# The temperature polynomial of an entropy-adaptive attention, moved from GpSimd to VectorE

## The reference, cut to what matters

```python
original_probs = softmax(logits)
entropy = sum(-original_probs * log(original_probs + 1e-09))      # one number for each query row and head
e2 = entropy * entropy
poly_result = POLY[0]*e2*e2 + POLY[1]*e2*entropy + POLY[2]*e2 + POLY[3]*entropy + POLY[4]
beta = where(entropy > 0.5, maximum(poly_result, 1.0), 1.0)
attn = softmax(logits * beta)
```

## Time and profile before

| | |
|---|---|
| median of 3 runs | 1427.24 us (1426.59 to 1428.86) |
| span of the profiled execution | 1426.1 us |
| PE busy | 1279.1 us, 90% |
| DVE busy | 781.4 us, 55% |
| ACT busy | 729.5 us, 51% |
| POOL busy | 531.3 us, 37% |

### The profile page before, as it was taken

One profiled execution on the slowest core, in us unless ns is written; L12 is line 12 of the kernel. 1 busy time (PEld: TensorE's weight loads), 2 busy tenths in 40 slices (PEclk: granted clock), 3 DMA queues, 4 the chain that ended last, 5 costly groups with the idle time before them and its releaser, 6 DMA issues. The chain is left out here.

```text
span 1426.1 us, 25147 instructions
## 1 busy us (share of the span) xinstructions
PE 1279.1 (90%) x9396; PEld 1061.4 (74%) x9396; DVE 781.4 (55%) x1807; ACT 729.5 (51%) x1297; POOL 531.3 (37%) x745
## 2 busy tenths in 40 slices
PE   9899999989999999996788889888888888999995
PEld 7576776757999999995555656656666556999995
DVE  4886878774111111112665688986877655533332
ACT  6464756652322233221456677778767656444441
POOL 2113040402000000004797888878769223332222
PEclk9999999999999999998998999999999999999998
DMA  9674472901977777822100011010010615322221
GB/s 349 269 184 130 114 183 71 259 25 52 321 259 262 268 268 261 326 105 84 41 1 4 9 42 34 1 38 20 12 38 20 250 55 185 61 43 49 41 44 12
DMA packets 71272, 170.81 MB, mean 120 GB/s; under 512 B 8572, under 2 KB 47489, under 8 KB 61168
## 3 DMA queue, kind: packets, MB, share of 16 engines
q1 hardware_dynamic: 55520, 144.33, 31.5%
q0 software_dynamic: 10224, 16.09, 4.9%
q10 hardware_dynamic: 5408, 8.78, 1.7%
HBM read 122.78 MB, written 48.07 MB: 120 GB/s over the span
## 5 line engine op out<-in xcount | busy, mean ns | idle before, releaser
L1198 ACT ACTIVATE b_ht<-ps,b_b 128x154 f32<-128x154 f32 x256 | 85.3, 387 | 200.5 <-PE ps L1165 187.0
L1213 DVE TENSOR_SCALAR b_yt<-ps,b_b 128x154 f32<-128x154 f32 x64 | 21.2, 373 | 238.8 <-PE ps L1178 238.8
L2353 POOL DMA_INDIRECT experts<-ye,gidx_all x32 | 32.0, 1000 | 319.8 <-SPq L1104 309.3
L1165 PE MATMUL ps<-b_xet,ring 128*128 128x154 f32 x1024 | 141.1, 295 | 1.0 <-DVE b_xet L1206 1.0
L1178 PE MATMUL ps<-b_ht,ring 128*128 128x154 f32 x1024 | 139.7, 294 | 0.4 <-DVE b_yt L1213 0.4
L1178 PEld LDWEIGHTS ps<-b_ht,ring 128*128 128x128 f32 x1024 | 136.3, 189 | 0.6 <-issue 0.6
L1165 PEld LDWEIGHTS ps<-b_xet,ring 128*128 128x128 f32 x1024 | 135.7, 189 | 1.1 <-DVE b_xet L1206 1.1
L2637 POOL DMA_INDIRECT out_dram<-d_yd,d_to x39 | 60.8, 1558 | 146.7 <-DVE d_yd L2605 119.5
L1538 DVE TENSOR_REDUCE c_mx<-ps 128x8 f32<-128x1024 f32 x64 | 77.7, 1214 | 51.9 <-PE ps L1482 51.9
L2586 DVE TENSOR_TENSOR d_g<-d_gs,ps 128x512 f32<-128x512 f32 x37 | 25.4, 688 | 122.3 <-PE ps L2523 122.2
L1477 PE MATMUL ps<-experts 64*128 64x512 f32 x256 | 77.1, 674 | 16.3 <-ACT experts L1574 6.8
(11 more groups left out here) (345 smaller groups left out, 2969.3 us busy)
## 6 DMA issues: line engine op xcount, KB each, us to landing
ring<-in_w SPq DMA_DIRECT2D x64, 1024.0 KB, 5.3
xd<-zero SPq DMA_DIRECT2D x6, 3120.0 KB, 24.8
a_kp<-in_ctx_k SPq DMA_DIRECT2D x8, 1024.0 KB, 17.0
d_xd<-xd SPq DMA_DIRECT2D x39, 130.0 KB, 2.4
xe<-zero SPq DMA_DIRECT2D x1, 4928.0 KB, 35.2
b_xe<-xe SPq DMA_DIRECT2D x32, 154.0 KB
ye<-b_ye ACTq DMA_DIRECT2D x32, 154.0 KB
experts<-in_wd SPq DMA_DIRECT2D x1, 4608.0 KB
```

Of the source, the lines that this page charges most:

```text
L1165: r = pe.matmul(ps[:, b, CAP * (m % 2):CAP * (m % 2) + CAP], w1r[:, slot, k, P * m:P * m + P], xet[:, e % 2, k, :], start=(k == 0), stop=( ...
L1198: r = a.activation(ht[:, e % 2, m, :], ps[:, b, CAP * (m % 2):CAP * (m % 2) + CAP], ACT.Gelu, bias=b1[:, e, m:m + 1])
```

## The change

The nine operations on POOL and their place "po" in the order are gone. DVE does six fused operations on the same 128x8 tiles, written directly behind the sum L1807 in step "hr", so without an own due time. The algebra is (h + a) h + b for each factor instead of a h + b + h h, and the factor POLY[0] or zero is taken into the second factor. The tile `square` is gone. All other due times and the order of everything else stay. `be` is now raised by DVE; POOL's "db" waits for it as before.

```diff
             def unit(u):
                 v.wait_ge(*pr.at(g, u))
                 v.tensor_reduce(h, e[:, :, :], AX, ALU.add).then_inc(*hr.up())
+                p, (other, chosen) = po[u][:, :], (x[:, :] for x in gt[u])
+                v.wait_ge(*hr.at(g, u))
+                v.scalar_tensor_tensor(out=p, in0=h, scalar=FACTORS[0][0], in1=h, op0=ALU.add, op1=ALU.mult)
+                v.scalar_tensor_tensor(out=other, in0=h, scalar=FACTORS[1][0], in1=h, op0=ALU.add, op1=ALU.mult)
+                v.tensor_scalar(chosen, h, -0.5, POLY[0], ALU.is_lt, ALU.mult).then_inc(*c.dv.up())
+                v.wait_ge(*c.dv.now())
+                v.scalar_tensor_tensor(out=other, in0=other, scalar=FACTORS[1][1], in1=chosen, op0=ALU.add, op1=ALU.mult).then_inc(*c.dv.up())
+                v.wait_ge(*c.dv.now())
+                v.scalar_tensor_tensor(out=p, in0=p, scalar=FACTORS[0][1], in1=other, op0=ALU.add, op1=ALU.mult).then_inc(*c.dv.up())
+                v.wait_ge(*c.dv.now())
+                v.tensor_scalar(p, p, 1.0, None, ALU.max).then_inc(*be.up())
...
             def unit(u):
-                yield at("po", u)
-                pool.wait_ge(*hr.at(g, u))
-                pool.tensor_tensor(square, h, h, ALU.mult)
-                pool.tensor_scalar(p, h, *FACTORS[0], ALU.mult, ALU.add)
-                pool.tensor_scalar(other, h, *FACTORS[1], ALU.mult, ALU.add).then_inc(*c.po.up())
-                pool.tensor_scalar(chosen, h, -0.5, POLY[0], ALU.is_lt, ALU.mult)
-                pool.wait_ge(*c.po.now())
-                pool.tensor_tensor(p, p, square, ALU.add)
-                pool.tensor_tensor(other, other, square, ALU.add).then_inc(*c.po.up())
-                pool.wait_ge(*c.po.now())
-                pool.tensor_tensor(p, p, other, ALU.mult).then_inc(*c.po.up())
-                pool.wait_ge(*c.po.now())
-                pool.tensor_tensor(p, p, chosen, ALU.mult).then_inc(*c.po.up())
-                pool.wait_ge(*c.po.now())
-                pool.tensor_scalar(p, p, 1.0, None, ALU.max).then_inc(*be.up())
                 yield at("db", u)
                 pool.wait_ge(*be.at(g, u))
                 pool.tensor_tensor(d, d, wide(po[u]), ALU.mult).then_inc(*db.up())
```

More of the change, by code:

```diff
@@ L1627, in phase_c @@
         zz, en, po = ([sb("%s%d" % (name, u), [P, NU]) for u in range(len(UNITS))] for name in ("zz", "en", "po"))
-        gt = [[sb("%s%d" % (name, u), [P, NU]) for name in ("square", "other", "chosen")] for u in range(len(UNITS))]
+        gt = [[sb("%s%d" % (name, u), [P, NU]) for name in ("other", "chosen")] for u in range(len(UNITS))]
         x_rot, x_rms = [sb("x_rot%d" % n, [P, GS, D]) for n in range(2)], sb("x_rms", [P, GS, D])
@@ L1815, in unit @@
                 e, l, d = ent[u % 2][:, :, :], lnp[u % 2][:, :, :], one.d[u][:, :, :]
-                h, p, (square, other, chosen) = en[u][:, :], po[u][:, :], (x[:, :] for x in gt[u])
+                h, p, (other, chosen) = en[u][:, :], po[u][:, :], (x[:, :] for x in gt[u])
                 yield at("pn", u)
```

## The result

The changed kernel takes 1455.83 us (median of 4 runs, 1452.24 to 1458.67) against 1427.62 us of the kernel before (1426.59 to 1428.86): ratio 1.0194, 95% interval 1.0176 to 1.0213. It is slower by 28.2 us; the forecast was +2.1 and the range ended at 1436.0. A second comparison gave 1455.98 us and a ratio of 1.0211 (1.0173 to 1.0249). A trace is one execution, and those profiled end layer 0's expert tiles (last L1213), which no edit touches, anywhere from 651.0 to 655.5 us. Where traces of different kernels are compared over the whole span, I therefore also give the time from that point to the end: 774.7 us before, 799.5 in the changed kernel (797.9 in its second profile), 24.8 us more.

The account below looks back on a forecast made before the run. Engines were taken to bound the stage in turns, mostly DVE from 830 to 939 and POOL to 991. Terms -0.3 + 0.85 + 7.15 - 5.0 - 0.6 = +2.1 us gave 1429.3 us, range 1421.7 to 1436.

Parts of the forecast that it names:

- The toll of one polynomial: Six small DVE operations behind each sum L1807: 1.0 us per polynomial, bounds 0.55 and 1.57, 32 us of DVE in all.
- the slow rival: Rival B, 28%: DVE becomes the bound; one small operation of 1.85 us on top gives 1436 us.
- 695 to 830, +0.55: First stretch: -0.3 from POOL's gain, +0.85 from two sums at 763.68 ahead of L1918, which waited 1.15 us.
- 830 to 939, +6.1 up to the mark: Mostly DVE's path: sums cost +2.0, +2.5 and +1.0, L1730 +1.65; together +7.15 us for the whole stretch.
- the side effect: L1730 near 901: without the polynomial POOL runs a product beside its four operations, 3.45 instead of 1.79 us, +1.65.
- 939 to 991, -5.0: POOL on the path with four polynomials, 9.8 us; waits for DVE and ACT leave half of the gain, -5.0.
- rival B: 28%: DVE bounds the stage, deciding when the product at 968.80 waits for the reciprocal (slack 1.84 us); 1433.9 to 1436 us.
- 991 to 1110, -0.6: Last stretch: sum at 1021.93 on DVE's path +1.0, one polynomial on POOL's path -1.6; other sums covered by DVE idle.
- What is behind 1110: After the stage: no polynomial, so everything moves as a block by the shift with which the stage ends.
- One sign that I had named for it: After the change DVE between 830 and 947 should show almost no idle time.
- A: Rival, 22%: POOL's queue is the bound and DVE has room; -5.5 us in all, 1421.7 us.
- C: Rival, 10%: the change does nothing, gain and toll within 1 us or both beside a third engine's chain; 1427 us.

Follow-up runs that it names:

- the runs with reciprocals: Changed kernel, polynomial left out, reciprocals of 128x8 in place of the six VectorE operations: six per sum 1442.48 us, three 1430.09 us, six at the later step 1432.61 us.
- no polynomial: Kernel before with the polynomial left out on every engine (the factor is 1): 1425.25 us, ratio 0.9971.
- six reciprocals: Changed kernel with each of the six new VectorE operations replaced by a reciprocal of 128x8 in the same place, polynomial left out: 1442.48 us, ratio 1.0116.
- the later place: Six operations as their own VectorE step at the due time of GpSimd's old polynomial: changed kernel so altered 1441.82 us; the six-reciprocals kernel so altered 1432.61 us.
- the run with all kinds: Kernel without the polynomial, plus six independent 128x8 VectorE operations behind each sum, one of each kind in rotating order, results unused: 1455.19 us in one run.
- the run with halves: Changed kernel with each of GpSimd's three 128x1024 products in a unit issued as two of 128x512: 1451.46 us, ratio 1.0170.

## Why the prediction was wrong

The direction I thought a little likelier than its opposite came true, the size did not; the miss is 26.5 us, and the time lies 19.8 beyond the range.

Three terms of the sum failed. The toll of one polynomial was put at 1.0 us, and catching makes it 1.7 on average. The sums that pay it were counted as about eight, the others being taken as covered by idle time on VectorE; the runs with reciprocals give 17 to 21. And of the 5.0 us that GpSimd was to give back between 939 and 991 nothing came, since it waited for VectorE there.

The start of a sum on VectorE (L1807 and its counterparts), against its start in the kernel before, read from the timelines. Between these marks lie my four stretches; "forecast" is the running sum of the prediction up to there.

| sum that stood at | forecast | no polynomial | six reciprocals | changed kernel |
|---|---|---|---|---|
| 703.00 | 0 | +2.3 | +2.5 | -0.6 |
| 842.57 | +0.6 | -3.4 | +0.4 | +7.6 |
| 935.36 | +6.7 | +3.0 | +13.6 | +19.0 |
| 1013.00 | +2.7 | -1.5 | +14.1 | +20.6 |
| 1102.00 | +2.1 | -5.2 | +14.1 | +21.5 |

The first row is noise: no polynomial stands ahead of that sum, and in the second profile of the changed kernel it is +4.6. Differences between neighbouring rows are safer: in each of them the two profiles of the changed kernel agree within 1.5 us.

**The toll of one polynomial: the lower part right, the whole wrong.** A chain that is not caught costs 0.97 us, the forecast was 1.0. But 22.3 us over 32 polynomials are another 0.70 on average, so the toll is 1.7 us, above the upper bound of 1.57 that I had given. This is the first failed step, and its evidence lay in the earlier trace rows: the copy of 1.85 us that I put down as one mishap, "for the slow rival". One more row of the kernel before beside it explains it (POOL):

```profile
928.93 1.90 POOL L1840 TENSOR_TENSOR experts<-experts,c_po 128x1024 f32<-128x1024 f32 x1
```

The copy started at 929.00 and ended with that product, at 930.83 beside 930.85. Two more of its kind lay in the same trace. I had the mechanism in hand for the 3.45 us of L1730 and applied it to four operations of 128x256 only, not to the 192 that the change adds.

**695 to 830, +0.55.** From 703.00 to the mark behind this stretch the kernel without a polynomial gives back 5.7 us, the one with reciprocals 2.1, and the changed kernel loses 8.2. So VectorE's own time costs 3.6 here, and without catches the stretch comes out a little below the forecast. The 10.3 us between the last two (8.9 with the second profile) are the catches, such as the three at 721 to 726. It is nearly all that they cost up to 1102.00: 13 of the 19, with 16.1 of the 22.3 us, lie ahead of this mark, and behind it the distance between the two columns does not grow (7.2 us at the mark, 7.4 at 1102.00).

**830 to 939, +6.1 up to the mark.** Measured +13.2 with the reciprocals and +11.4 after the change. Without any polynomial it is already +6.4: the side effect, of which I counted 1.65 us at L1730, has 3.6 there, and as much falls on the routing's three operations, less 1.7 for the copy of the earlier trace rows, which isn't caught there. In the changed kernel the same work shows (DVE and POOL):

```profile
911.88 5.39 DVE L1730 SCALAR_TENSOR_TENSOR x_all<-experts,gwt_all,x_all 128x256 f32<-128x256 f32 x4
912.06 2.06 POOL L1836 TENSOR_TENSOR experts<-experts,c_po 128x1024 f32<-128x1024 f32 x1 [1.30 <-DVE c_po L1818]
914.08 2.52 POOL L1833 TENSOR_TENSOR experts<-experts 128x1024 f32<-128x1024 f32 x1
...
940.77 2.24 DVE L447 TENSOR_TENSOR c_ohs<-c_oh 128x32 bf16<-128x32 f32 x1
```

It was foreseen as "over 3 us" and is 5.39: two products catch it, one after the other, where the neighbour in the earlier trace rows had met one. This term was right in kind and too small by 2 us, and its like in the routing was missing. The rest, 13.2 - 6.4 = 6.8 us, is the tolls, for which I had 4.5 up to the mark.

**939 to 991, -5.0.** The gain exists: without a polynomial this stretch gives back 4.5 us (+3.0 to -1.5). With any toll on VectorE it is gone (+0.5 with the reciprocals, +1.6 after the change). The point of decision that I had named for rival B is the one that decided: GpSimd waits for L1804 (DVE and POOL of the changed kernel):

```profile
988.64 0.20 DVE L1804 RECIPROCAL c_zz<-c_zz 128x8 f32<-128x8 f32 x1
...
988.94 1.89 POOL L1830 TENSOR_TENSOR experts<-experts,c_zz 128x1024 f32<-128x1024 f32 x1 [3.94 <-DVE c_zz L1804]
```

The slack of 1.84 us, read at 966.76 in the earlier trace rows, was used up by a VectorE that came into the stretch 19 us late and not 7.

**991 to 1110, -0.6.** Without a polynomial -3.7, with the reciprocals 0.0, after the change +0.9. Here too the tolls take what GpSimd gives.

**What is behind 1110** does not move quite as a block: the mark at 1102.00 is 21.5 late, the span grew by 24.4; without a polynomial it is -5.2 and -2.8. So some 2 to 3 us are added in the tail in both; with the reciprocals it is 0.3.

**The rivals.** B named the mechanism of the second part, VectorE as the bound, and the place where it decides; at 1434 to 1436 it was priced with eight or nine paid places. Reciprocals cost 17 to 21 us more than no polynomial, at 1.0 each: 17 to 21 of the 32 sums pay, if each pays in full. One sign that I had named for it did not come: VectorE has 104.40 us busy of the 117 from 830 on, 105.81 before, so it still idles there. It sets the pace through what waits for it (GpSimd's product 52.5 us behind L1804), and not by being full. A and C are refuted: GpSimd's whole polynomial is worth 4 us.

In all, in ratios of the kernel before taken of 1427: without the polynomial -4; six operations on VectorE at the later place +9; at the place right behind the sum instead +12; caught by GpSimd's products +11; sum +28. Each term has some 4 to 5 us of uncertainty. The medians would divide them otherwise (own time +10, place +7, catches +15), and so would the traces from the end of layer 0's experts on (-3, +5, +11, +12, sum +25).

**What stays open.** Why the later step is worth 7 to 12 us without any catch was not shown. In its trace other work of VectorE stands between the sum and the six at 28 of the 32 sums, the row maximum L1538 at 15 of them; that this is what pays is only argued. The share of TensorE's lower clock was not separated either, and it is a rival for a part of every term: PE's busy time is 1278.8 us without a polynomial, 1286.8 with the reciprocals and 1293.7 in the changed kernel.

## What to carry to other kernels

Before a small operation goes to VectorE while GpSimd works, look for small copies and products in the trace that take 10 times their usual time, and lay GpSimd's rows beside them: here one such row was a rule, not a mishap. Price an added operation as its own time plus the chance of being caught times what is left of GpSimd's instruction then (1.2 us on average here), for the old operations too when GpSimd's gaps close. Count the places that pay generously: here that was as large an error as the catches. An engine that looks idle half of the span (ScalarE here, with a form of the polynomial that suits it) can be the better taker than the one that looks fast.

## What the hardware showed that I had not expected

- A VectorE operation of 128x8 that reads and writes SBUF and is of a kind that can be caught waits for the end of the GpSimd product that runs at its start, up to 2.2 us for a work of 0.15: 19 of 192 in the changed kernel, 29 of 192 in the run with all kinds.
- The kind decides: two-tensor, scalar-tensor-tensor, tensor-scalar, copy and cast operations are caught; reciprocal (0 of 192 in the kernel with six, 15 of them right at the start of the chain beside a product) and sum (L1802 and L1807, 19 of 64 beside a long GpSimd operation) are not.
- A chain of dependent small operations can be caught several times in a row (three of the six at 721 us here, five in the run with halves), since each one frees GpSimd's next instruction to go first. Halving GpSimd's instructions did not lessen the sum: 22.3 us in 19 against 23.5 in 25.
- GpSimd's products are hardly longer for it: 2.06 and 2.52 us beside L1730, where 1.90 and 2.36 are usual.
